# Masks on VectorE, a redrawn order of TensorE's work and an earlier release of its banks, and a fold of attention moved by one step

## The reference

```
# layer 0, attention: (B, T, D) = (2, 2048, 256), 16 heads, each with two maps (q, k of 8 columns, v of 16)
att = einsum('bhtd,bhsd->bhts', q, k) * scale;  att = where(causal, att, -inf);  att = softmax(att)
att = att[:, :, 0] - lambda_full * att[:, :, 1]
out = einsum('bhts,bhsd->bhtd', att, v);  out = rmsnorm(out) * gamma * (1 - LAMBDA_INIT);  x += out @ w_proj + experts

# layer 1, state space: inner width 512, 16 states
xc, z = split(x @ in_proj);  xs = silu(causal_conv(xc));  dt_r, B, C = split(xs @ x_proj);  dt = softplus(dt_r @ dt_proj + b)
h[t] = exp(dt * A) * h[t-1] + dt * B[t] * xs[t]            # over 2048 tokens
y = (einsum('btis,bts->bti', h, C) + xs * D_skip) * silu(z);  a = y @ out_proj
# layer 1, sign network: 512 -> 1024 -> 1024 -> 256, weights +1 or -1
f = s2 * (relu(s1 * (relu(s0 * ([x, -x] @ W0)) * 2 @ W1)) * 2 @ W2);  x += a + f
```

## Time and profile before

| | us |
|---|---|
| median of 3 runs | 3645.06 (3644.28 to 3647.44) |
| the profiled execution's own time | 3652.44 |
| its span, first to last instruction | 3650.7 |
| PE busy, share of the span | 3371.8 (92%) |
| DVE busy | 2740.1 (75%) |
| ACT busy | 2215.3 (61%) |
| POOL busy | 1517.1 (42%) |

### The profile page before, as it was taken

How to read it: one execution, slowest core, us unless ns; L and a number is a source line. 1 busy time by engine, 2 the same in 40 slices (tenths; PEclk the granted TensorE clock), 3 DMA queues, 4 the chain that set the end, 5 groups by cost and what they waited for, 6 DMA issues and landing times. The chain is left out here.

```text
span 3650.7 us, 61127 instructions
## 1 busy us (share of the span) xinstructions
PE 3371.8 (92%) x20642; PEld 1445.0 (40%) x20655; DVE 2740.1 (75%) x4442; ACT 2215.3 (61%) x3459; POOL 1517.1 (42%) x1879
## 2 busy tenths in 40 slices
PE   8998999989999999999999999768998998989987
PEld 5564666643333333333333333342333333333332
DVE  4654223468888888888888888356888888888898
ACT  3431221147777777777777777537766766767663
POOL 2225000013323333333233333207777777777786
PEclk9999999989999999999999999888999999999999
DMA  4443111101111111111111100132222222222121
GB/s 153 136 147 109 45 46 44 41 29 39 51 42 38 34 32 28 29 33 34 34 34 31 33 26 21 53 105 64 70 63 77 67 64 70 65 76 71 64 73 53
DMA packets 160890, 211.70 MB, mean 58 GB/s; under 512 B 32324, under 2 KB 108364, under 8 KB 160604
## 3 DMA queue, kind: packets, MB, share of 16 engines
q1 hardware_dynamic: 141340, 172.51, 15.6%
q0 software_dynamic: 8512, 18.76, 1.6%
q10 hardware_dynamic: 10752, 16.78, 1.4%
HBM read 154.48 MB, written 52.69 MB: 57 GB/s over the span
## 5 line engine op out<-in xcount | busy, mean ns | idle before, releaser
L1319 DVE TENSOR_REDUCE pmax<-psR 128x1 f32<-128x512 f32 (+3 forms) x2170 | 1318.2, 669 | 159.6 <-PE psR L1374 92.3
L1265 ACT ACTIVATE prob<-psS 128x1024 f32<-128x1024 f32 (+3 forms) x1280 | 1099.9, 905 | 337.3 <-PE psS L1427 329.5
L2088 POOL TENSOR_TENSOR hc<-h_d,crep 128x512 f32<-128x512 f32 x512 | 648.5, 1271 | 254.5 <-DVE h_d L2306 204.5
L1374 PE MATMUL psR<-kslab,qslab 48*128 48x512 bf16 (+3 forms) x2480 | 677.3, 353 | 45.5 <-DVE pmax L1319 20.9
L1427 PE MATMUL psS<-qslab,kslab 51*128 51x512 bf16 (+3 forms) x2560 | 643.6, 351 | 4.9 <-ACT prob L1265 4.4
L1442 PE MATMUL psVo<-prob,vaug 128*32 128x512 f32 (+3 forms) x5120 | 625.0, 544 | 0.9 <-ACT ov L1269 0.9
L1197 POOL TENSOR_SCALAR_AFFINE_SELECT prob<-prob 128x256 f32<-128x256 f32 (+1 forms) x512 | 208.7, 420 | 782.8 <-ACT prob L1265 782.4
L2296 DVE TENSOR_TENSOR psU<-dtx,psX 128x512 f32<-128x512 f32 x512 | 356.2, 696 | 179.4 <-PE psX L2462 105.3
L2306 DVE TENSOR_TENSOR_SCAN h_d<-a,state,psU 128x512 f32<-128x512 f32 x384 | 489.3, 1274 | 0.0
L1374 PEld LDWEIGHTS psR<-kslab,qslab 48*128 48x128 bf16 x2480 | 185.3, 93 | 721.4 <-DVE pmax L1319 534.1
L2213 ACT ACTIVATE a<-dt,a_neg 128x512 f32<-128x512 f32 x512 | 364.8, 720 | 57.8 <-DVE h_d L2306 56.4
(11 more groups left out here) (293 smaller groups left out, 4859.4 us busy)
## 6 DMA issues: line engine op xcount, KB each, us to landing
crep<-c_rows_d SPq DMA_DIRECT2D x256, 256.0 KB, 3.1
x_e<-rows_d SPq DMA_DIRECT2D x72, 128.0 KB, 2.0
y_d<-y SPq DMA_DIRECT2D x72, 128.0 KB, 1.7
q_d<-parts SPq DMA_DIRECT2D x48, 128.0 KB
k_d<-parts SPq DMA_DIRECT2D x48, 128.0 KB
qslab<-q_d SPq DMA_DIRECT2D x60, 96.0 KB
kslab<-k_d SPq DMA_DIRECT2D x60, 96.0 KB
x<-in_L_attn_x_dram SPq DMA_DIRECT2D x8, 512.0 KB, 5.8
```

The costliest lines, as they stand in the source:

```text
L1265: act.activation(prob[g % BUFS][:, :, off:BLK], psS[g % 2][:, :, off:BLK], ACT.Exp).then_inc(prob_ready, 1)
L1319: dve.tensor_reduce(pmax[:, a].rearrange("p i c -> p (i c)")[:, lo:lo + (count - 1) * NEXT + 1:NEXT], psR[at % BANKS][:, 0:count * w].rear ...
L1374: ins = pe.matmul(dst[:, m * w:(m + 1) * w], qslab[u][rows, i * P:(i + 1) * P], kslab[u][rows, ch * BLK:ch * BLK + w], start=(m == 0), sto ...
L2088: pool.tensor_tensor(hc[:, g % CR], h[:, g % HR], crep[:, g // PAIR % SPR], ALU.mult).then_inc(hc_ready, 1)
```

## The change

Three parts. In attention, max items with one masked part are no longer masked by PE: DVE adds a bias (bias_d, 0 or -1e30, made once by POOL in the expert stage) and takes the maximum in one tensor_tensor_reduce, which also writes the sum to a spare tile. FOLD is LAG + 4, so folds are in odd steps (7, 11, 19, 31), behind the max items and ahead of the value products. In the state-space stage the table is redrawn, sums of l3 and out are read by DVE one unit earlier, and keep_state comes after ACT's copies; some of ACT's and POOL's units move with the table.

```diff
@@ phase_experts, gpsimd
+            c.after(pool.memset(keep["bias_d"][:], 0.0))
+            c.after(pool.affine_select(out=keep["bias_d"][:, BLK - P:BLK], in_=keep["bias_d"][:, BLK - P:BLK],
+                                       compare_op=ALU.is_ge, fill=NEG, base=0, pattern=[[-1, P]], channel_multiplier=1))
@@ phase_attention
-        FOLD = LAG + 3
+        FOLD = LAG + 4
+        bias_d = keep["bias_d"]
+        spare = [sb(f"spare{s}", [P, BLK]) for s in range(BANKS)]
@@ take_max
+                if masked and count == 1:
+                    dve.tensor_tensor_reduce(spare[at % BANKS][:, 0:w], psR[at % BANKS][:, 0:w], bias_d[:, BLK - w:BLK], 1.0, NEG,
+                                             ALU.add, ALU.max, into[:, lo:lo + 1]).then_inc(ring_free[at % BANKS], 1)
+                    return
@@ max_products
-                if not masked:
+                if not (masked and len(parts) > 1):
                     ins.then_inc(ring_full, 1)
@@ max_mask
-                if not masked:
+                if not masked or len(parts) == 1:
                     return
@@ pieces
-            for f, at in enumerate((0, 2, 4, 6, 10, 13, 15, 17) if blk else (0, 2, 8, 9, 10, 13, 15, 17)):
+            for f, at in enumerate((0, 2, 5, 7, 11, 13, 15, 16) if blk else (0, 2, 8, 9, 10, 11, 12, 13)):
                 put("l1", f, at, [4])
-                put("out", 0, 8, [2, 2, 2, 2])
-                put("out", 1, 13, [2, 2, 2, 2])
+                put("out", 0, 6, [4, 4])
+                put("out", 1, 9, [4, 4])
             put("l2", 0, 18, [4, 4, 4, 4])
-            for f in range(1, FT):
-                put("l2", f, 18 + 4 * f, [6, 5, 5])
-            put("l3", 0, 52, [6, 6, 5, 5, 5, 5])
-            put("l3", 1, 58, [6, 6, 5, 5, 5, 5])
+            for f in range(1, 4):
+                put("l2", f, 17 + 5 * f, [5, 4, 4, 3])
+            for f, at in enumerate((37, 41, 45, 49)):
+                put("l2", 4 + f, at, [6, 5, 5])
+            put("l3", 0, 53, [6, 7, 6, 7, 6])
+            put("l3", 1, 58, [7, 6, 7, 6, 6])
-                for e, at in enumerate(((5, 7, 12, 16) if blk else (12, 14, 15, 16)) + (49, 51, 53, 55)):
+                for e, at in enumerate(((4, 9, 12, 14) if blk else (14, 15, 16, 17)) + (48, 52, 56, 60)):
                     put("xz", e, at, [2])
-                for c in range(CT):
-                    put("cv", c, 20 + 4 * c, [2, 2])
-                put("xd", 0, 36, [2, 2])
-                for c in range(PAIR):
-                    put("dt", c, 41 + 4 * c, [1])
+                for c, at in enumerate((17 if blk else 19, 23, 28, 33)):
+                    put("cv", c, at, [1, 1, 1, 1])
+                put("xd", 0, 38, [1, 1, 2])
+                for c, at in enumerate((44, 46)):
+                    put("dt", c, at, [1])
@@ phase_state_space, scalar
-                if g:
-                    keep_state(g - 1)
                 if t:
                     for kind, e, lo, hi in PLAN[blk][t - 1]:
...
+                if g:
+                    keep_state(g - 1)
@@ phase_state_space, vector
-                if t == 1 and blk:
-                    sign_out(blk - 1, 1)
...
-                if t >= 2:
-                    for kind, e, lo, hi in PLAN[blk][t - 2]:
+                if t >= 1:
+                    for kind, e, lo, hi in PLAN[blk][t - 1]:
```

More of the change, by code:

```diff
@@ L1314, in take_max @@
                 count, lo = len(parts), BPB * i + ch
+                into = pmax[:, a].rearrange("p i c -> p (i c)")
                 at = PLACE[("max", n, x)]
@@ L1318, in take_max @@
                 dve.wait_ge(ring_full, at + 1 + CREDIT)
-                dve.tensor_reduce(pmax[:, a].rearrange("p i c -> p (i c)")[:, lo:lo + (count - 1) * NEXT + 1:NEXT],
+                if masked and count == 1:
+                    dve.tensor_tensor_reduce(spare[at % BANKS][:, 0:w], psR[at % BANKS][:, 0:w], bias_d[:, BLK - w:BLK], 1.0, NEG,
+                                             ALU.add, ALU.max, into[:, lo:lo + 1]).then_inc(ring_free[at % BANKS], 1)
+                    return
+                dve.tensor_reduce(into[:, lo:lo + (count - 1) * NEXT + 1:NEXT],
                                   psR[at % BANKS][:, 0:count * w].rearrange("p (n w) -> p n w", w=w), AX.X, ALU.max)\
@@ L2099, in _ @@
                         cut_x(blk + 1, (t - 31) // 2)
[L2100 to L2103, removed]
+                    if t in (42, 44):
+                        rest(blk + 1, (t - 42) // 2)
                     if t in (52, 54):
-                        scaled_input(blk + 1, (t - 52) // 2)
+                        step_size(blk + 1, (t - 52) // 2)
+                    if t in (53, 55):
+                        scaled_input(blk + 1, (t - 53) // 2)
         @block.scalar
@@ L2260, in _ @@
                 if blk + 1 < NBLK:
-                    if t in (27, 35):
-                        silu_conv(blk + 1, (t - 27) // 8)
-                    if t == 27 and blk == 0:
+                    if t in (28, 38):
+                        silu_conv(blk + 1, (t - 28) // 10)
+                    if t == 28 and blk == 0:
                         silu_gate(0)
@@ L2266, in _ @@
                         copy_x(blk + 1)
-                    if t in (39, 41, 43):
-                        cut_bc(blk + 1, (t - 39) // 2)
-                    if t == 47:
+                    if t in (41, 43, 45):
+                        cut_bc(blk + 1, (t - 41) // 2)
+                    if t == 49:
                         log_exp(blk + 1, 0)
-                    if t == 48:
+                    if t == 50:
                         log_term(blk + 1, 0)
-                    if t == 57:
+                    if t == 62:
                         silu_gate(blk + 1)
@@ L2369, in _ @@
                             add_out(blk - 1, e)
-            sign_out(NBLK - 1, 1)
             gate(NBLK - 1, 1)
@@ L2553, in build @@
                 keep["fold"] = side("fold", [P, 2, OC], F32)
+                keep["bias_d"] = side("bias_d", [P, BLK], F32)
                 keep["lam_in"] = side("lam_in", [P, 4, HD], F32)
```

## The result

The changed kernel takes 3662.24 us (median of five, 3660.29 to 3664.55) against 3647.44 (median of five, 3644.28 to 3648.31) for the kernel before: ratio 1.0038, 95% interval 1.0026 to 1.0049. The forecast of 3600 and its range of 3560 to 3648 are both missed, on the other side. The profiled execution took 3662.24 us with a span of 3660.5, against 3652.44: +9.8.

The account below looks back on a forecast made before the run. DVE's maxima bound attention; in the state-space stage DVE's input terms and scans, plus waits for PE. Attention +28 and state-space -73 gave -45: 3652.44 to 3607, 3600 as the median (7.4 lower); range 3560 to 3648.

Parts of the forecast that it names:

- Masks: Attention, 496 masked maxima moved to DVE: +30 us for the operation, -23 for mask waits gone, -4 for PE.
- read-out rival: Attention, masked maxima: the maximum is read out separately, +49 us over the forecast, 3649, no change; chance 0.07.
- two-cycle rival: Attention, masked maxima: the new operation takes two cycles a column, 0.59 us each, 294 us instead of 30, 3864; chance 0.08.
- PE's saved time: Attention: some 992 short mask products leave PE, mostly where it waits for DVE anyway; 4 us, between 0 and 15.
- the price of +0.16: Attention, masked maxima: a separate short step for the maximum costs +0.16 us each, so masks cost 79 us instead of 30.
- The fold: Attention, fold moved to the odd step: DVE starves 1.15 us instead of 0.78; +0.8 a head, +25 us, bounds -15 and +50.
- The even plan: State-space stage, redrawn table, earlier reads and block start together: -73 us, bounds -27 and -100.
- Block start: State-space stage: second residual sum taken in unit 63, dt product's bank free, -2.0 us a block; clock no longer falls, -12.
- Even quarters: State-space stage: convolution and l2 products spread over more units, stalls at 26, 30, 34 and 38 shrink, -4.2 us a block.
- Bank waits: State-space stage: out products moved, sums read earlier, ACT copies first; stalls at units 14 to 24 shrink, -2.5 us a block.
- the fold pays: Attention: PE is the bound around folds more often, so the move saves bank stalls; -25 instead of +28, 3547; chance 0.13.
- the plan empties only the block start: State-space stage: interleaving fp32 convolution with f16 products costs what spreading wins; -27 instead of -73, 3646; chance 0.12.

## Why the prediction was wrong

**What bounds the kernel** was read rightly: in attention DVE's maxima set the pace and PE's lateness near folds costs in full. The result is that reading with a larger lateness.

**Masks: +3 forecast (30 - 23 - 4), -5 measured.** Two errors nearly cancel here, which is luck. The operation costs 0.01 us more than the reduce where I took 0.06 from the 726 ns row, 5 us instead of 30; so the read-out rival and the two-cycle rival both fall. And the waits for masks did go, 24.7 us for the 23 forecast, but 16.2 of them came back as waits for max products, a term that the sum did not have: 5 - 24.7 + 16.2 = -3.5, and attention is 4.5 us shorter by its exponentials. For PE's saved time, put at 4, nothing is left. The Trainium skill, VectorE: DVE Perf Modes, section Two Vector instructions with no wait between them, counts an operation with an accumulator output as two instructions. The trace agrees: 496 read-outs of 83 ns. But the price of +0.16 that I had tied to that rule is not there, because the second instruction runs beside the next one. The Trainium skill, Vector Engine (DVE) Microarchitecture Reference, section Points that are easy to get wrong, has the throughput of an accumulating two-operand form halved with two sources in SBUF that are not bf16. Here one source is a bank, and 684 ns show nothing halved; no run has both sources in SBUF, so none tests the rule itself.

**The fold: the step that failed.** The prediction said "I take +0.8 us a head, 31 x 0.8 = +25 us; bounds -15 (only the saved changes) and +50." It was +80 and +86. Two terms were wrong.
- The size of the wait. I reckoned 1.15 us of starvation (the terms as written add up to 1.17), on the ground that the fold finds two unread items, and said of the fold beside the turn only "so more", without a number. That one is 0.91 us more than before (1.95 us where the clock stays, against 0.80 + 0.24), and the next most costly, the fold of step 19, has its value products 3.84 us apart instead of 3.10, +0.74. The two in steps 7 and 11 cost next to nothing together. By the heads' lengths it is 1.5 us a head instead of 0.8, so 47 us instead of 25, just inside my upper bound. DVE's idle, over 1 us behind each fold by the forecast, is 0.91 us at step 7, 0.69 at 11, 1.35 at 19 and 1.95 at 31.
- The clock, which had no term at all. I looked at the clock only where the trace of before showed it low, in the other stage. In attention have it at 0.99. The change itself made a place where PE waits (0.30), turns (0.27), waits (0.33) and folds, and at that place the granted clock fell to 0.50, that is 1.2 GHz, in most heads. That is the other 41 us, beyond the bound. That the fold ahead of the value products in an odd step brings the falls is shown: they are gone with it behind them, or in an even step. Which of the short waits does it is not: heads with the same waits have no fall, and the fold of step 7, without a turn, has falls too.

With both, +86 in the place of +25, the sum would have come to about +16 and the right side. With the waiting alone, +47, it would have come to -23, still faster and inside the range: it is the clock that took the time out of it.

**The even plan: -73 forecast, -67 in the trace, -63 alone.** Nearly right as a sum and in its split. Block start with the clock: 2.0 x 7 + 12 = 26 forecast, 28 measured. Even quarters: 4.2 a block, seven blocks, 29 forecast, 22 measured. Bank waits: 2.5 a block, some 17 forecast; the order on ACT gave 7, and the rest of it is the untried part. Two details were wrong. There are still stretches at 0.50 at the starts of blocks, 47.7 us at six of the seven starts against 92.3 at all seven before, where I had said none. And the stalls did not vanish but sit at units 6 to 10 (up to 2.08 us in blocks 1 to 6, counted from 0); those of units 26, 30 and 34 are gone, but for 0.83 us at unit 26 of two blocks. DVE's wait for B, 42.0 us, lies in the forecast 30 to 45, and the first seven blocks take 133.6 to 138.8 us against 133 to 136; the seventh 135.9, from 144.8.

**The rivals.** That the fold pays was wrong by its sign. That the plan empties only the block start is refuted by the 22 us of the even table. The slower side had 0.10 of the chances and hung on the price of an instruction; it came from the fold instead, which I had bounded too narrowly.

## What to carry to other kernels

- An engine that works in order holds everything behind an instruction that waits. Put what needs a bank from the bottleneck engine behind the work that needs nothing from it: 64 of the 86 us came back by swapping two calls in one step.
- When the bottleneck engine is fed by another one, count the longest stretch in which the feeder makes nothing for it. Two such pieces of 1 us in one step cost; in neighbouring steps they were hidden. Price every instance of a moved step, the most crowded one first.
- Moved work can lower PE's clock where it never fell before, although PE was never idle for more than 0.35 us at a time in the heads of the changed kernel. A clock of 0.99 in the profile before is no promise, and a clock term belongs in the upper bound of every edit that adds waits on PE.

## What the hardware showed that I had not expected

- The clock falls at a definite place of a repeated pattern in one head and not in another. In the changed kernel the stretches at 0.50 begin at 1223.3, 1274.5, 1325.7, 1376.9 and on to 1786.5 us, once a head, each 3.4 us; heads at 1118.3, 1168.3 and 1885.9 with the same instructions have none and take 50.0 us instead of 51.2. The cost is 1.2 us for 3.4 at half clock, 2.8 for 6.8, and 4.2 to 5.5 for 10.2.
- The kernel that falls in some heads only has the widest spread: 25 us over ten runs with the turn moved, 4 us over ten with the masks alone.
- The tensor_tensor_reduce over a bank and an fp32 tile, with a full output beside the maximum, runs at the speed of a plain reduce (684 ns for 512 columns), and its accumulator read-out of 83 ns hides beside the next operation.
